# One 256-row iteration of the shared expert moved in front of the routed blocks

## What is computed

```python
x = x + _L0_attn_ref(_layernorm(x), ...)
h = _layernorm(x)                                   # 1024 x 256
probs = softmax(h @ gate_w.T)                       # 8 experts, the best 2 per token
out_e = (silu(h @ fc1[e].T) * (h @ fc2[e].T)) @ proj[e].T       # 176 wide, routed
shared = (silu(h @ shared_fc1.T) * (h @ shared_fc2.T)) @ shared_proj.T   # 704 wide, all tokens
x = x + sum_e combine[:, e] * out_e + sigmoid(h @ shared_gate_w.T) * shared
x = x + _L1_attn_ref(_layernorm(x), ...)
x = x + _L1_ffn_ref(_layernorm(x), ...)
```

## Time and profile before

| | us |
|---|---|
| median of three runs | 849.47 |
| lowest and highest | 849.12, 849.98 |
| the profiled execution's own time | 845.31 |
| its span, first to last instruction | 843.5 |
| TensorE busy in the span | 792.2 (94%) |
| VectorE busy | 482.7 (57%) |
| ScalarE busy | 361.2 (43%) |
| GpSimd busy | 218.0 (26%) |
| mean granted TensorE clock | 0.986 |

### The profile page before, as it was taken

How to read it: one execution, slowest core, us unless ns; L and a number is a source line. 1 busy time by engine, 2 the same in 40 slices (tenths; PEclk the granted TensorE clock), 3 DMA queues, 4 the chain that set the end, 5 groups by cost and what they waited for, 6 DMA issues and landing times.

```text
span 843.5 us, 14393 instructions
## 1 busy us (share of the span) xinstructions
PE 792.2 (94%) x4825; PEld 548.0 (65%) x4825; DVE 482.7 (57%) x1166; ACT 361.2 (43%) x756; POOL 218.0 (26%) x318
## 2 busy tenths in 40 slices
PE   5998799879989998899999999989999999999998
PEld 3576566666657786677777767766765545455557
DVE  5999866766522226866565565757745373324443
ACT  3988777646113324352232342323256676211111
POOL 3644654111610034111112111116712233200000
PEclk9988999999989999999999999999999999999999
DMA  4001780082253322033542322212333423293431
GB/s 143 2 1 28 225 299 2 2 222 85 89 162 102 100 69 63 26 103 121 140 135 68 101 67 68 75 38 91 111 80 113 137 88 121 68 291 128 125 126 50
DMA packets 95807, 85.72 MB, mean 102 GB/s; under 512 B 34792, under 2 KB 84456, under 8 KB 95736
## 3 DMA queue, kind: packets, MB, share of 16 engines
q1 hardware_dynamic: 88200, 70.05, 28.3%
q0 software_dynamic: 4224, 11.74, 4.0%
q10 hardware_dynamic: 3312, 3.02, 1.1%
HBM read 57.02 MB, written 26.71 MB: 99 GB/s over the span
## 4 chain that ended last, share of the span: by engine, by line
PE 73%; DVE 11%; ACT 6%; issue 6%; POOL 2%; DMA 2%; SPq 0%; ACTq 0%; DVEq 0%; POOLq 0%
PE bank L1488 9%; PE bank L1451 7%; PE bank L1345 6%; PE bank L1306 6%; PE bank L1331 6%; PE bank L1267 5%; PE bank L1283 5%; PE bank L730 4%; PE bank L756 3%; PE bank L953 3%; PE bank L2309 3%; PE bank L975 2%; PE bank L2266 2%; PE bank L2293 2%; POOL rows_in L1205 2%
## 5 line engine op out<-in xcount | busy, mean ns | idle before, releaser
L1607 ACT ACTIVATE arena<-bank 128x512 f32<-128x512 f32 (+1 forms) x96 | 46.9, 525 | 148.5 <-PE bank L1451 148.5
L1229 POOL TENSOR_TENSOR arena<-arena,causal_t 128x256 f32<-128x256 f32 x64 | 45.1, 726 | 218.1 <-ACT arena L1612 218.0
L1488 PEld LDWEIGHTS bank<-arena 128*128 128x128 f32 x640 | 76.2, 191 | 4.3 <-POOL arena L1229 2.9
L1488 PE MATMUL bank<-arena 128*128 128x129 f32 x640 | 77.1, 275 | 1.7 <-POOL arena L1229 1.7
L1451 PE MATMUL bank<-arena 128*128 128x512 f32 (+3 forms) x256 | 76.2, 442 | 1.4 <-DVE arena L1685 1.4
L1540 ACT ACTIVATE arena<-bank 128x512 f32<-128x512 f32 (+1 forms) x39 | 20.2, 521 | 118.1 <-PE bank L1267 108.3
L1306 PE MATMUL bank<-arena 128*128 128x256 f32 (+1 forms) x272 | 67.9, 389 | 2.5 <-DVE arena L1665 2.4
L1267 PE MATMUL bank<-xnT,arena 128*128 128x512 f32 (+1 forms) x168 | 65.8, 514 | 0.5 <-issue 0.5
L1306 PEld LDWEIGHTS bank<-arena 128*128 128x128 f32 (+1 forms) x272 | 52.0, 194 | 21.2 <-issue 10.7
L1345 PE MATMUL bank<-arena 128*128 128x256 f32 x256 | 61.0, 381 | 2.7 <-DVE arena L1692 2.0
L1345 PEld LDWEIGHTS bank<-arena 128*128 128x128 f32 x256 | 48.1, 190 | 23.6 <-issue 12.8
(11 more groups left out here) (296 smaller groups left out, 1491.6 us busy)
## 6 DMA issues: line engine op xcount, KB each, us to landing
arena<-in_w_gu SPq DMA_DIRECT2D x44, 256.0 KB, 3.7
rows_in<-place SPq DMA_DIRECT2D x5, 1664.0 KB, 14.6
arena<-in_w_dn SPq DMA_DIRECT2D x34, 128.0 KB, 3.5
rows<-arena SPq DMA_DIRECT2D x8, 544.0 KB, 4.6
arena<-in_w_dn SPq DMA_DIRECT2D x24, 176.0 KB
arena<-in_wq SPq DMA_DIRECT2D x32, 128.0 KB, 3.1
arena<-in_wo SPq DMA_DIRECT2D x32, 128.0 KB, 2.0
arena<-rows SPq DMA_DIRECT2D x32, 128.0 KB, 2.1
```

What stands on the lines that cost most here:

```text
L1229: nc.gpsimd.tensor_tensor(blocks, blocks, causal_t[:].unsqueeze(1).to_broadcast([P, 2, P]), ALU.mult).then_inc(s_p, 1)
L1488: mm = nc.tensor.matmul(b_o[pair][:, t * (DH + 1):(t + 1) * (DH + 1)], pr[:, o:o + P], v[:, grp, kt, :], start=(kt == 0), stop=(kt == qb))
L1607: nc.scalar.activation(th[:, sbank * 512:sbank * 512 + w], b_s[sbank][:, 0:w], ACT.Tanh, scale=SCALE / SOFTCAP).then_inc(s_th, 1)
```

## The change

Iteration 7 (tile 1 over 256 tokens) moves ahead of the blocks: `F0B` becomes 8 (the name `F0H1`, 6, is untouched). Since iteration 7 uses banks 0 and 1, the blocks now start with banks 4 and 5: their gate/up pair becomes (4, 0) and the down product moves to bank 5. `PAIRS` is reordered so that the iterations behind the blocks meet the banks in the order in which they come free. One wait is rewritten with the same value, 12.

```diff
-    F0H1, F0B, F0END = T0, T0 + AHEAD, 2 * T0 + T0 - AHEAD
+    F0H1, F0B, F0END = T0, T0 + AHEAD + 1, 2 * T0 + T0 - AHEAD
...
-    assert (MOE[0][0] * MOE[0][2] + MOE[0][3]) % P == HT and thin(F0B - 2) and not thin(F0B - 1)
+    assert (MOE[0][0] * MOE[0][2] + MOE[0][3]) % P == HT and thin(F0H1 - 1) and IT[F0B - 1][4] == 256
...
-    PAIRS = [5, 0, 4, 1]
+    PAIRS = [1, 4, 0, 5]
...
-    b_x, b_gu, b_h, b_yb = bank[2], (bank[0], bank[4]), bank[3], bank[1]
+    b_x, b_gu, b_h, b_yb = bank[2], (bank[4], bank[0]), bank[3], bank[5]
...
-                    dve.wait_ge(s_pd, F0B + T0 - AHEAD)
+                    dve.wait_ge(s_pd, 2 * T0)
```

## The result

The changed kernel took 844.69 us (median of 9 runs, 841.79 to 847.78), the kernel before 849.34 beside it (9 runs, 848.34 to 850.06): a ratio of 0.9948, 95% interval 0.9928 to 0.9968. That is 4.4 us (849.34 x 0.0052) where 1.25 was forecast, and the time lies outside the range. Its profiled execution, the fastest of the nine, took 841.79 with a span of 840.0.

What follows compares the result with a forecast made beforehand. TensorE was taken as the bound, with block 3's load setting the blocks' time. -0.15 + 1.5 - 2.60 = -1.25 us against the profiled 845.31, carried over to the median 849.47, gave 848.2, range 846.3 to 849.9.

Steps and rivals of the forecast that it cites:

- Part 3: Behind the new hole before turn(3): the clock falls to half for one short stretch, +1.5 us, bounds 0 and 3.42.
- Part 1: TensorE ahead of block 3: the hole before turn(0) goes, TensorE is ready for turn(3) 3.4 us earlier.
- Part 2: Block 3's load, issued 0.97 us later, flies 2.2 us; turn(3) moves by -0.15 us, bounds -0.37 and +0.96.
- Rival C: At turn(3): block 3's load isn't the bound, TensorE's 3.4 us come through; -6.0 us, 843.5; chance 0.03.
- Rival B: Behind the new hole: the clock holds or falls too late to cost much; -2.75 us, 846.7; chance 0.27.
- Part 4: Behind the blocks: iteration 7's gate, up and down leave TensorE's list, -2.60 us, bounds -2.60 and -0.7.
- Rival F: Behind the blocks: the gathers hold the end, leaving only -0.7 there; +0.65 us in all, 850.1; chance 0.07.

Runs made afterwards that it cites:

- b_again2: The kernel before, unaltered, run again on chip 1: 845.0 us, ratio 0.9998 to the kernel before there.
- a_again3: The changed kernel, unaltered, run again on chip 1: 845.64 us, ratio 1.0012 to the kernel before there.
- b_again: The kernel before, unaltered, run again on chip 14: 849.17 us, ratio 1.0002 to the kernel before there.
- a_again: The changed kernel, unaltered, run again on chip 14: 845.94 us, ratio 0.9948 to the kernel before there.
- after: The changed kernel's profiled execution in the first measurement, fastest of its nine: 841.79 us, where the runs' median is 844.69.
- a_spall2: Changed kernel with the loads of tiles 8 to 11 moved behind blocks 6, 8, 10 and 12, repeated on chip 8: 839.07 us, 0.9926 of before.
- a_tail: Changed kernel plus three unread 512-column matmuls (2.6 us) behind block_down(22), chip 14: 848.92 us, 0.9986 of the kernel before.
- a_fillend: Changed kernel plus three unread matmuls (512, 512, 256 columns) ahead of down(15), chip 3: 846.04 us, 0.9942 of the kernel before.
- a_spall: Changed kernel with the loads of tiles 8 to 11 moved behind blocks 6, 8, 10 and 12, chip 3: 842.87 us, 0.9905 of before.
- b_fillend: Kernel before plus three unread matmuls (512, 512, 256 columns) ahead of down(15), chip 3: 848.12 us, 0.9985 of the kernel before.
- b_plain2: Kernel before with its sixteen indirect gathers replaced by plain DMAs of the same size, chip 15: 845.55 us, 0.9953 of the kernel before.
- b_fill: Kernel before plus three unread 512-column matmuls ahead of block_turn(0), chip 14: 848.56 us, 0.9979 of the kernel before.

## Why the prediction was wrong

The two pairs of traces of unaltered kernels, one chip each, side by side (us between the starts of the named work, read from TensorE in order of time):

| | forecast | chip 1: b_again2 to a_again3 | chip 14: b_again to a_again |
|---|---|---|---|
| turn(3) | -0.15 | 247.88 to 247.73: -0.15 | 247.25 to 247.23: -0.02 |
| turn(3) to turn(4) | +1.5 | 2.49 to 4.26: +1.77 | 2.49 to 2.58: +0.09 |
| block_down(22) to down(15) | -2.60 | 24.28 to 21.58: -2.70 | 24.99 to 23.02: -1.97 |
| down(15) to scores(0) | 0 | 12.11 to 11.96: -0.15 | 15.18 to 13.56: -1.62 |
| start of scores(0) | -1.25 | -1.24 | -3.52 |
| rest of the span | 0 | +1.69 | -0.15 |

**The step that failed** is, first, the last one of the sum: "The runs' median, 849.47, is 4.2 us above the profiled one, of which no row tells the cause; I carry the difference over to it". The difference wasn't a constant on top. It was late semaphores and 6.83 us of half speed behind the blocks, which the profiled execution doesn't have: 40.17 us from block_down(22) to scores(0) in b_again against 36.39 in b_again2, so 3.8 more. The changed kernel has only 3.0 more of it in a_again and 1.8 in `after` (36.58 and 35.34 against the 33.54 of a_again3): a part of the 4.2 goes with the change. Second, on chips of that kind part 3's +1.5 fails: +0.09 between b_again and a_again. By these single executions the two pairs differ by 2.28 us at scores(0): 1.68 of it from part 3, 0.74 from behind the blocks, less 0.13 at turn(3). Seen from a chip of the first kind the change is worth 4.4 us, of which the pair of traces shows 3.5; on a chip like the profiled one, nothing that can be measured (0.9997 and 1.0012).

**Part 1** was right: TensorE is at turn(0) at 239.01 in `after` and 239.51 in a_again3 (forecast 239.51), and the hole before it is gone. In a_again TensorE comes later (242.19), behind a wait of 2.25 before down(4) and half speed from 230.2; the wait before turn(3) takes that up.

**Part 2** was right in the load's place and size: block 3's load, issued 1 us later against the issue of block 0, flies 2.29 us in `after` and 2.12 in a_again3. That turn(3) moves by just -0.15 on chip 1 is in part luck: in b_again and b_again2 it has no wait for rows at all, and comes straight from TensorE's own work, slowed by the stretch from 237. In the trace of the forecast that wait was 0.14, so there rows and TensorE were due at almost the same time. The Trainium skill's rule on small pieces (DMA: Bandwidth & Descriptors, Specifications), read as the prediction reads it (twice the bytes), would have given a flight of 3.31: the traces don't bear that out for 128 KB ahead of a load. Rival C, the end of the front hole coming through, was wrong for this change, but a_spall2 shows how much lay there: with no weight load in front of block 3's, both the wait and the half speed behind it go.

**Part 3** was right on chips 8 and 1, where all four kernels with this front pay 1.4 to 1.8 us behind turn(3). On the first kind it was mostly wrong: `after`, a_again and a_tail pay nothing (2.57, 2.58, 2.57 from turn to turn), a_fillend pays. Two things lie behind that. In a_again, a_tail and a_spall there is no hole to pay for: TensorE reaches turn(3) with a wait of 0.00, 0.11 and 0.00. It is late there since it waited 2.15 to 2.27 us before down(4), behind late semaphores at 222 to 229, and the clock fell behind that wait, from 229.9 to 230.7. All five traces with such a wait have that stretch (b_fillend and b_plain2 too); in the others the wait is 1.54 or less and the stretch isn't there. That it is this wait that brings it is read from these traces, no run altered it. In `after`, on the other hand, the clock holds behind a hole of 2.48 us, and in a_fillend it falls behind 2.19: why is open. Rival B's result is thus true of the predicted kernel's runs on this kind, its cause only of `after`.

**Part 4** was right on the second kind (-2.70). On the first the late semaphores hold it at -2.0: the addition after down(11) comes at 317.88 in `after`, 15.6 us after block_down(22), where a_again3, with the same work, has it 14.2 after (319.29). TensorE's wait for VectorE, which was to move as a whole (1.65), is 2.34 in `after` and 1.59 in a_again3. The other half of the gain there, -1.6, was in no part: the half-speed stretch behind down(15) shrinks from 6.83 to 3.41 in a_again and isn't there in `after`. a_tail, with the work back, has the 6.83 again. Rival F's wait for the gathers exists (1.2 us) and is absorbed, as said.

**What no part saw** is the other chip's +1.69: the stretch at half speed near 557, in the second layer, is 6.83 us long from 555.2 in a_again3 and 3.41 from 558.6 in b_again2. I had the row for it and took it as fixed. With it, the -1.24 becomes +0.45 in these two executions. The stretch is 0, 3.41 or 6.83 in traces of kernels that do the same work there, and of one and the same kernel (0 in `after`, 3.41 in a_again, 6.83 in a_again3), so single executions say little on it. By the runs' mean clock the change has fewer stretches on the first kind (0.985 to 0.990 on chip 14, each short stretch being 0.002) and slightly more on the second (0.9885 to 0.987 on chip 1).

**A better version** came out: a_spall is 0.9905 and 0.9926 of the kernel before on a chip of either kind (six runs each), where the changed kernel is 0.9948 and 0.9997.

## What to carry to other kernels

If the profiled execution lies outside the spread of the runs, as 845.31 did beside 849.12 to 849.98, it may show another case than the one you are asked about: look for what could make the difference before you carry it as a constant. When work is moved into a wait, look at what that wait is for: here it was for a load that stood behind nine others, and taking those out of its way gave 6 us where the move gave nothing, and 3 to 4 on top where the move gave 4.4. The half-speed stretches of one and the same kernel differ from execution to execution by 3.4 us and more, so a change of 1 to 2 us on paper needs the clock of several executions.

## What the runs showed of the hardware

- The kernel before takes 849.3, 849.25 and 849.37 us on three chips, 845.05 and 844.97 on two: 4.3 us (0.5%) apart. On the three, ScalarE and VectorE start up to 2.39 us after the matmul that they wait for, around indirect scatters and gathers; with plain DMAs of the same size in place of the gathers, none of them does behind the blocks (b_plain2).
- The half-speed stretches followed here were 3.41 or 6.83 us long. Most stand behind waits of TensorE of 2.15 to 3.21 us, and not behind each of them: 2.40 us before down(15) was followed by 6.83 us of it in b_again, 2.34 by none in `after`. In two traces one of 3.41 us began within a microsecond of the end of a wait of only 1.06 (from 240.54 in b_fillend, 240.13 in b_plain2, both with an earlier stretch at 230).
- A load behind 128 KB in pieces of 256 bytes, issued 0.76 us after them, flew 2.29 us (`after`) and 2.12 (a_again3), near the 1.98 of one with nothing ahead of it (block 0 in the first trace of before) and far from 3.31.
